# Expert slots in two phases: nine complete tiles of the first four groups, listed by GpSimd in step 15, run behind the last ranks

## The reference

```python
x = x + ga * attn(h)       # bidirectional state-space block: projection, causal convolution,
                           # scan over 2048 tokens forward and backward, gate, norm, out_proj
h = _layernorm(x) * (1 + cb) + sb
gate_logits = einsum('bsd,ed->bse', h, gate_w) + gate_b + expert_bias
top_idx = argmax(gate_logits, axis=-1)          # one of 8 experts per token
for e in range(8):
    mask = (top_idx == e)[..., None]
    y = relu(h @ w1[e] + b1[e]) @ w2[e] + b2[e]   # 128 -> 512 -> 128
    out = out + mask * y
x = x + gb * out
```

## Time and profile before

| | us |
|---|---|
| median of 3 runs | 446.13 (444.88 to 448.41) |
| the profiled execution's own time | 446.73 |
| its span in the trace | 444.8 |
| PE busy in the span | 400.8 (90%), 3156 instructions |
| DVE busy | 354.7 (80%) |
| ACT busy | 290.8 (65%) |
| POOL busy | 317.0 (71%) |

### The profile page before, as it was taken

The page is one execution under the profiler, slowest core; times in us unless marked ns, Lnnn a source line. Parts: engine busy times, 40 slices in busy tenths (PEclk is TensorE's granted clock), DMA queues, the critical chain, the costliest instruction groups (busy, mean ns, idle before and its releaser), DMA issues.

```text
span 444.8 us, 10736 instructions
## 1 busy us (share of the span) xinstructions
PE 400.8 (90%) x3156; PEld 364.5 (82%) x3156; DVE 354.7 (80%) x1064; ACT 290.8 (65%) x827; POOL 317.0 (71%) x478
## 2 busy tenths in 40 slices
PE   7898989997998899798998998999988699999990
PEld 7676878897898698587898887899877699999990
DVE  5758789998879999988889987996987078778781
ACT  3748699787699897787788789987420044444430
POOL 4744894899995989589898898697575245656662
PEclk9869999999999999999999999999999999999997
DMA  8999999999800000010101100031112578888740
GB/s 233 323 335 335 334 336 332 334 336 332 256 7 0 2 2 0 1 49 2 50 1 49 37 13 1 1 117 75 49 36 74 170 206 222 234 221 224 214 146 0
DMA packets 54856, 63.30 MB, mean 142 GB/s; under 512 B 4604, under 2 KB 47868, under 8 KB 54672
## 3 DMA queue, kind: packets, MB, share of 16 engines
q1 hardware_dynamic: 49808, 54.57, 41.4%
q0 software_dynamic: 2832, 6.50, 4.1%
q10 hardware_dynamic: 2160, 1.55, 1.3%
HBM read 20.97 MB, written 42.09 MB: 142 GB/s over the span
## 4 chain that ended last, share of the span: by engine, by line
PE 35%; DVE 17%; issue 12%; POOL 12%; ACT 10%; DMA 5%; SPq 5%; ACTq 2%; POOLq 0%; DVEq 0%
PE bank L1351 3%; PE bank L1302 3%; POOL out_dram L856 3%; PE bank L1367 3%; PE bank L1371 3%; PE bank L1344 3%; DVE bank L1778 3%; PE bank L1363 3%; POOL routed_rows L768 2%; PE bank L1329 2%; SPq L536 2%; POOL accb L637 2%; SPq L530 2%; DMA zs<-routed_rows 2%; PE bank L1335 2%
## 5 line engine op out<-in xcount | busy, mean ns | idle before, releaser
L637 POOL TENSOR_TENSOR accb<-accb,prod 128x512 f32<-128x512 f32 x48 | 61.3, 1278 | 29.2 <-ACT accb L949 25.5
L1778 DVE SCALAR_TENSOR_TENSOR bank<-raw,cw,bank 128x512 f32<-128x512 f32 x96 | 72.1, 751 | 2.3 <-ACT bank L959 0.9
L856 POOL DMA_INDIRECT out_dram<-raw x39 | 38.2, 979 | 34.3 <-POOL raw L851 12.8
L673 POOL TENSOR_SCALAR lseg<-strict,av 128x128 f32<-128x128 f32 x128 | 48.0, 388 | 6.8 <-DVE av L1737 4.8
L1351 PE MATMUL bank<-skip,cx 128*128 128x128 f32 x256 | 41.1, 283 | 7.0 <-DVE st L1824 6.6
L1212 ACT ACTIVATE raw<-bank 128x128 f32<-128x128 f32 x39 | 10.8, 278 | 53.4 <-PE bank L1575 47.8
L1239 PE MATMUL bank<-ones 128*128 128x128 f32 x266 | 38.8, 296 | 5.2 <-issue 2.7
L1603 PE MATMUL bank<-raw 128*128 x312 | 43.1, 282 | 0.0
L998 ACT ACTIVATE xt<-bank,dtv 128x128 f32<-128x128 f32 x128 | 39.5, 362 | 5.5 <-PE bank L1330 5.2
L768 POOL DMA_INDIRECT routed_rows<-rows,rowat x32 | 32.8, 1025 | 14.1 <-issue 8.6
L1351 PEld LDWEIGHTS bank<-skip,cx 128*128 128x128 f32 x256 | 33.6, 191 | 9.8 <-DVE st L1824 9.0
(11 more groups left out here) (238 smaller groups left out, 1148.4 us busy)
## 6 DMA issues: line engine op xcount, KB each, us to landing
routed_rows<-padrow SPq DMA_DIRECT2D x32, 1040.0 KB, 12.6
zs<-in_w_dram SPq DMA_DIRECT2D x35, 258.0 KB, 3.3
zs<-routed_rows SPq DMA_DIRECT2D x39, 130.0 KB, 3.2
raw<-in_w_dram SPq DMA_DIRECT2D x1, 2048.0 KB, 7.6
xs<-in_u_dram SPq DMA_DIRECT2D x3, 512.0 KB, 9.7
routed_rows<-padrow SPq DMA_DIRECT2D x8, 130.0 KB, 3.4
zs<-in_w_dram ACTq DMA_DIRECT2D x4, 258.0 KB, 4.6
out_dram<-raw POOLq DMA_INDIRECT x39
```

The lines of the kernel that those rows point to most:

```text
L637: pool.tensor_tensor(accb[:, :], accb[:, :], prod[:, :], ALU.add).then_inc(s_tapb, 1)
L673: last = pool.tensor_scalar(lseg[:, Q % LA, h, :], strict[:, d, :], av[:, b, col(d, h, t)], 1.0, ALU.mult, ALU.mult)
L856: pool.indirect_dma_start(out_rows, bass.IndirectOffsetOnAxis(ap=tok[:, s % 4, :].bitcast(mybir.dt.uint32), axis=0), ob[:, s % 4, :], None ...
L1778: dve.scalar_tensor_tensor(out=acc(S, g)[:, :], in0=raw[:, g, c0:c0 + BLK], scalar=cw[:, d, g, k:k + 1], in1=acc(S, g)[:, :], op0=ALU.mult ...
```

## The change

`FIRSTG` is 4 and `K1` is 9: of the 2048 tokens of groups 0 to 3, whatever the routing, at least ceil((2048 - 8 x 127) / 128) = 9 tiles of some expert are full. These nine tiles become slots 0 to 8 (first phase), the other 30 (`K2`) slots 9 to 38 (second phase).

- **POOL** gets `first_table()` in step 15, third chunk, ahead of `forward_norms(LASTG, 0, 2)`: 13 operations each of which waits for the one before (`link_first`) and three that don't, which list the nine tiles from `nextrow` as it stood after group 3. `table_constants` has six operations in place of three. `taken_tiles()`, five operations, stands between the last scatter of group 5 and those of group 6; it tells DVE's table which tiles are already taken. Behind the scatters POOL waits for all nine tiles of rows, copies their token numbers at once, and issues nine puts (`s_put1`) ahead of the 30 others.
- **SP** waits for `s_yz` as before, then for `s_firstv` and for the scatters of groups 0 to 3 alone, loads nine tiles of rows and, between them, w1 of slots 0 to 3, then w1 of slots 4 to 8. Then it waits for `s_tabv`, loads w1 of slots 9 to 12, waits for all scatters, and loads the rows of slot 9 and on. `RR` is 13. ACT issues no w1 any more.
- **PE** runs two `turn_rows` and four products of ones ahead of `ranks(7)`, then `hidden(0)` and slots 0 to 8, then waits for table and rows of slot 9, and goes on as before. The 44 products of ones of the three constants, and five ahead of `ranks(7)`, are gone. Slots 0 to 2 use one pair of PSUM banks (4, 5) for the hidden blocks; slot 3 and later ones alternate between two pairs. In the first phase the transposes and the sums of `down` share banks 0 and 3.
- **ACT** does all four hidden blocks of slots 0 to 8, and copies their sums to SBUF (`keep_sum`).
- **DVE** has a table of 30 slots in place of 39, and behind it works on the first nine outputs in wide operations (`first_gates`, `first_outputs(0, 4)` and `first_outputs(4, 9)`). It rectifies from slot 9 on.
- w1 lies in `hT` (three places) and `zs` (one), the nine sums and gates in `yzb`. The second `yT` transposes of group 7 use the alternating side banks in place of bank 0.

```diff
 # POOL, step 15
                     if j == 2:
+                        first_table()
                         forward_norms(LASTG, 0, 2)
                         scatter(g2)
...
             scatter(LASTG - 2, 3, BT)
+            taken_tiles()
             scatter(LASTG - 1)
             scatter(LASTG)
+            for s in range(K1):
+                hold(pool, s_rb[s], 16)
+            pool.tensor_copy(tok1, rr[:, 0:K1, 2 * DM:2 * DM + 1]).then_inc(s_tok, K1)
...
+            for s in range(K1):
+                put(s)
+            for s in range(K1, NSLOT):
                 token_numbers(s)
-                if s >= 1:
+                if s > K1:
                     put(s - 1)
 # POOL, the list (cut)
+            def first_table():
+                wide = [P, K1, NE]
+                first = prefix[:, 0, NE // 2:]
+                hold(pool, s_tab, NTAB0)
+                hold(pool, s_rt_dve, NR * (FIRSTG - 1) + 5)
+                link_first(pool.tensor_tensor(whole, nextrow[:, FIRSTG % 2, :], region_mid, ALU.subtract))
+                link_first(pool.tensor_scalar(whole, whole, 1.0 / P, ROUND, ALU.mult, ALU.add))
+                link_first(pool.tensor_scalar(first, whole, ROUND, 1.0, ALU.subtract, ALU.mult))
+                pool.tensor_scalar(coef[:, 0], first, -float(P), float(REGION), ALU.mult, ALU.add)
...
+                link_first(pool.tensor_tensor(behind1[:, 0], behind1[:, 1], coef[:, 0].unsqueeze(1).broadcast_to(wide),
+                                              ALU.mult))
...
+                pool.tensor_copy(slot_r[:, :, 0:K1], last).then_inc(s_firstv, 1)
 # SP
-            sp_.wait_ge(s_yz, NCH)
-            sp_.wait_ge(s_tabv, 1)
+            sp_.wait_ge(s_yz, CHUNKS + TPB + ZUSED)
...
+            sp_.wait_ge(s_firstv, 1)
+            landed(sp_, FIRSTG)
+            for s in range(K1):
+                first = first_row(s)
+                load_rows(s, first)
+                if s < RW:
+                    load_w1(s, first)
+            for s in range(RW, K1):
+                load_w1(s, first_row(s))
+            sp_.wait_ge(s_tabv, 1)
+            ahead = [first_row(s) for s in range(K1, K1 + 2)]
+            for s in range(K1, K1 + RW):
+                load_w1(s, ahead[s - K1] if s < K1 + 2 else first_row(s))
+            landed(sp_, B * NBLK)
             sp_.wait_ge(s_pad, 16)
             sp_.wait_ge(s_fresh[NFRESH], 16 * NE)
-            load_rows(0, first0)
...
+            for s in range(K1, NSLOT):
+                first = ahead[s - K1] if s < K1 + 2 else first_row(s)
                 load_rows(s, first)
-                load_w1(s, first)
+                if s >= K1 + RW:
+                    load_w1(s, first)
 # ACT
+            for s in range(NACT, K1):
+                if s + 1 < K1:
+                    rectify(s + 1, 0)
+                    if s + 2 < K1:
+                        rows_T(s + 2)
+                    rectify(s + 1, 1)
+                keep_sum(s)
 # PE
+            pe.wait_ge(s_firstv, 1)
             pe.wait_ge(s_yz, NCH - 1)
...
             logits(LASTG)
-            keep_warm(bank[4], 5)
-            ranks(LASTG)
-            keep_warm(bank[4], WARM_TABLE)
...
-            pe.wait_ge(s_tabv, 1)
-            keep_warm(bank[4], WARM_SCATTER)
...
-            keep_warm(bank[4], WARM_ROWS)
...
             turn_rows(0)
             turn_rows(1)
+            keep_warm(bank[4], 4)
+            ranks(LASTG)
             hidden(0)
-            for s in range(NSLOT):
+            for s in range(NPE, K1):
+                if s + 1 < K1:
+                    hidden(s + 1)
+                    if s + 2 < K1:
+                        turn_rows(s + 2)
+                down(s)
+            pe.wait_ge(s_tabv, 1)
...
+            turn_rows(K1)
+            turn_rows(K1 + 1)
+            hidden(K1)
+            for s in range(K1, NSLOT):
 # DVE
+            def first_outputs(s0, s1):
+                dve.wait_ge(s_yo2, s1)
+                link_early(dve.tensor_tensor(ob1[:, s0:s1, :], ob1[:, s0:s1, :], gsel1[:, s0:s1, :], ALU.mult))
+                dve.tensor_tensor(ob1[:, s0:s1, :], ob1[:, s0:s1, :], rr[:, s0:s1, DM:2 * DM], ALU.add).then_inc(s_ob, s1 - s0)
...
+            first_gates()
+            first_outputs(0, K1 // 2)
+            first_outputs(K1 // 2, K1)
+            rectify_high(K1)
```

More of the change, by code:

```diff
@@ L43 @@
 W1C = FF + FC
-RR = 6
+FIRSTG = 4
+K1 = -(-(FIRSTG * BLK - NE * (P - 1)) // P)
+assert 2 < K1 <= FIRSTG * BLK // P
+ROUND = 1.5 * 2.0 ** 23
+RR = 13
 RW = 4
+assert K1 <= RR
 B2K = 96
@@ L1194, in _, with rows_T, rectify, keep_sum @@
                         softplus_exp(nxt)
+            def rows_T(s):
+                act.wait_ge(s_eT, s + 1)
+                if s >= 2:
+                    act.wait_ge(s_h1, s - 1)
+                act.activation(hTs[:, s % 2, :], turn_bank(s)[:, 0:P], ACT.Copy).then_inc(s_eTc, 1)
+            def rectify(s, half):
+                act.wait_ge(s_h1a if half == 0 else s_h1, s + 1)
+                if s >= 2:
+                    act.wait_ge(s_y2, s - 1)
+                for f in range(half * FC // 2, (half + 1) * FC // 2):
+                    c0 = (f % 2) * P
+                    last = act.activation(hr[:, s % 2, f * P:(f + 1) * P], bank[high_low(s) + half][:, c0:c0 + P],
+                                          ACT.Relu, bias=w1t[s % RW][:, FF + f:FF + f + 1])
+                last.then_inc(s_hra if half == 0 else s_hrb, 1)
+            def keep_sum(s):
+                act.wait_ge(s_y2, s + 1)
+                act.activation(ob1[:, s, :], sum_bank(s)[:, 0:DM], ACT.Copy).then_inc(s_yo2, 1)
             out_T(LASTG, 0)
@@ L1534, in _, with turn_rows, hidden @@
                         sums(nxt)
+            def turn_rows(s):
+                pe.wait_ge(s_rb[s % RR], 16 * (s // RR + 1))
+                if s >= 2:
+                    pe.wait_ge(s_eTc, s - 1)
+                if 3 <= s < K1:
+                    pe.wait_ge(s_yo2, s - 2)
+                elif s in (K1, K1 + 1):
+                    pe.wait_ge(s_yo2, K1)
+                pe.transpose(turn_bank(s)[:, 0:P], rr[:, s % RR, 0:DM], ident[:, :]).then_inc(s_eT, 1)
+            def hidden(s):
+                pe.wait_ge(s_eTc, s + 1)
+                pe.wait_ge(s_w1[s % RW], 16 * (s // RW + 1))
+                if s == 0:
+                    pe.wait_ge(s_yz, NCH)
+                if s == 3:
+                    wait_free(pe, USE["o", LASTG, 0])
+                    wait_free(pe, USE["o", LASTG, 1])
+                for f in range(FC):
+                    if s not in (0, 3) and f == 0:
+                        pe.wait_ge(s_hra, same_banks(s) + 1)
+                    if s not in (0, 3) and f == FC // 2:
+                        pe.wait_ge(s_hrb, same_banks(s) + 1)
+                    c0 = (f % 2) * P
+                    mm = pe.matmul(bank[high_low(s) + f // 2][:, c0:c0 + P], w1t[s % RW][:, f * P:(f + 1) * P],
+                                   hTs[:, s % 2, :], start=True, stop=True)
+                    if f == FC // 2 - 1:
+                        mm.then_inc(s_h1a, 1)
+                mm.then_inc(s_h1, 1)
```

278 lines of the change are left out of this document (160 added, 118 removed).

## The result

The changed kernel took 449.29 us at the median (447.77 to 452.19, 8 runs), the kernel before 446.72 us beside it (8 runs, 444.88 to 453.27): ratio 1.0059, interval 1.003 to 1.0088. The forecast was 435.0 us, the range 432 to 440. It was wrong, by 14 us.

The account below looks back on a forecast made before the run. PE was taken to bound the 39 slots at 2.01 us each. First transpose of the rest +6.8 us, nine fewer slots behind it -18.1, net -11.3 from 446.73: 435.4, or 434.8 at the median, given as 435; range 432 to 440.

Parts of the forecast that it names:

- The pace of phase one: Slots 0 to 8: PE sets the pace at 2.01 us a slot; bounds 2.01 to 2.3, that is 0 to +2.
- rival B: Phase one slower, from w1 late beside the scatters or ACT falling behind: +2 to +4, about 438 us; chance 0.11.
- The joint between the phases: Before slot 9: rows queue behind SP's w1 of slot 12; PE stands 2.7 us, first transpose at 360.9.
- Rival D: At the joint, PE's clock falls to half during its stand: +5, 438 to 444 us; chance 0.10.
- GpSimd's list: Step 15 on POOL: `first_table` takes 5.4 to 5.6 us inside 5.82 us idle; taken as 0, bounds 0 to +1.
- rival C: Step 15: the list on POOL overruns its idle time because DVE holds it up, 436.5 to 439 us; chance 0.09.
- The sharing of banks at the start: Slots 0 to 2 share one pair of banks, so `hidden(1)` waits for ACT; costs about 1.5 us.
- w1 beside the scatters: Phase one's w1 loads arrive in time, 1.1 us to spare in the worse case; taken as nothing, bounds 0 to +3.
- A: Whole kernel: the forecast itself holds, 433 to 437.5 us; chance 0.60.
- F: At the joint: no stand, the rest starts at 358.2, 2.7 us better, 432.5 us; chance 0.03.
- G: Phase one: the nine slots wait for what they should run ahead of, work only moved, about 446 us; chance 0.03.
- E: Behind the joint: clock stays low, kernel slower by 1% from 8 half-clock slots, 455 us with ten; chance 0.04.

Follow-up runs that it names:

- value_early: Changed kernel with TensorE's load of the slot's expert number moved ahead of the transpose: 434.25 us, ratio 0.9751 to the kernel before.
- after: The changed kernel's own profiled execution, the slowest of its eight runs: 452.19 us, span 450.5; median 449.29 us, ratio 1.0059 to the kernel before.
- again: The changed kernel, unchanged, measured once more beside the kernel before: 438.94 us, ratio 0.9854.
- both_2: The program of both, unchanged, in another set of runs, a quiet set: 430.88 us, ratio 0.9671 to the kernel before.
- value_early_2: The program of value_early, unchanged, in a late set: 448.65 us, ratio 1.0034 to the kernel before.
- fill_joint: value_early with nine products of the constant block on TensorE behind `down(8)`: 446.28 us, ratio 0.998 to the kernel before.
- quiet set: Runs measured together, no kernel waiting over 0.5 us on "remote", with more DMA landing records (3209 to 3338); kernel before 444.6, 444.8 and 445.7 us.
- late set: Runs measured together, all but the kernel before waiting over 0.5 us on "remote", with fewer DMA landing records (2111 to 2226); kernel before 447.8 and 448.6 us.
- both: value_early with the rows of slots 9 to 12 all issued ahead of their four w1, in a late set: 447.59 us, ratio 1.0018 to the kernel before.
- both_swap: both with GpSimd's `first_table()` moved behind the last group's two norms and ahead of the scatter: 454.99 us, ratio 1.0171 to the kernel before.
- spaced: both with one GpSimd addition ahead of each of the last eight scatters and the nine puts issued one per slot: 443.27 us, ratio 0.9898.
- before_2: The kernel before, unchanged, run for its trace in a late set: 449.93 us (one run).

## Why the prediction was wrong

Four points of TensorE's timeline cut the forecast and the traces into the same pieces, in us. The forecast's transpose of slot 8 is its end of `down(8)`, 358.2, less the 4.2 us that lie between the two in value_early.

| | hidden(0) at | to transpose 8 | to transpose 9 | to the end | span |
|---|---|---|---|---|---|
| forecast | 338.7 | 15.3 | 6.9 | 72.6 | 433.5 |
| after | 340.9 | 24.2 | 9.1 | 76.3 | 450.5 |
| again | 338.2 | 18.2 | 7.8 | 74.5 | 438.6 |
| value_early | 336.6 | 15.3 | 7.0 | 73.8 | 432.6 |
| both_2 | 337.3 | 15.2 | 4.7 | 72.5 | 429.7 |
| value_early_2 (late) | 338.5 | 22.8 | 9.3 | 75.3 | 445.9 |

**The step that failed first is "The pace of phase one".** It said that PE needs 2.01 us a slot, and bounded the pitch by 2.01 to 2.3. The queue of matrix instructions was counted; the sequencer's was not. The load of the expert number had always been there at no cost. The change put a wait ahead of it, and I asked what is queued behind that wait only among the products. Measured: 2.50 to 2.65 us a slot, 2.9 us over the stretch (15.3 to 18.2), and nothing once the load moved ahead of the wait. That was rival B's size (+2 to +4), with another cause than the two it named: neither w1 nor ScalarE's load was late.

**"The joint between the phases" was right, and incomplete.** SyncE's order, the rows' DMA as releaser and a stand of 2.7 us (measured 2.78 in after, 3.12, 2.76) came as written. Rival D, given 0.10, came on top of it in each of the nine kernels that stood there for 2.7 to 3.3 us with nothing to fill the stand: half clock behind it. From transpose 9 to transpose 13 both_2 takes 5.7 us at full clock, value_early 7.3 and again 8.4 (364.14 to 372.58). So it costs 1.7 us where it lasted 3.4 us (value_early) and 2.8 us where it lasted 6.8 us (again), and 1.3 and 2.0 us by the time from transpose 9 to the end, where D had +5. TensorE: Matmul & The Clock Gate (the Trainium skill, What's actually happening) put it under 1% of a span; 0.4 to 0.6% is measured, and the trace agrees. My evidence against D, the stretch from 350 to 354, was sound as a reading: the kernel before had stood there for 2.67 us, as long as at the joint, and kept the clock.

```profile
351.76 1.58 PE L1239 MATMUL bank<-ones 128*128 128x128 f32 x12 [2.67 <-issue]
```

It misled as a forecast for the joint, where all nine were followed by half clock; what makes the difference is not shown. With products of ones in the stand (fill_joint, one execution) the clock stayed.

In a quiet set these two terms nearly close the account. again's span is 5.1 us over the forecast's 433.5: 2.9 in phase one, 0.9 up to transpose 9 (0.5 one more load, 0.4 a longer stand), 1.9 behind it, less 0.5 at `hidden(0)`. value_early, which has the pitch right, lies 0.9 under 433.5 and inside the range, but that is luck: its `hidden(0)` came 2.1 us early, for a cause that no run shows. both_2 lies 3.8 under, 2.2 of it the stand that the forecast had counted in and 1.4 at `hidden(0)`.

**The larger part of the miss in the measurement itself was in no step and no rival.** The forecast put the delay of TensorE's signals to ScalarE and VectorE at what a quiet trace shows, everywhere. Of the 17.0 us by which the profiled span exceeds 433.5, 2.3 were there at `hidden(0)`. Of 8.9 us up to transpose 8, the pitch explains 2.9 by again; 6 are the wait on "remote" and the half clock from 347.7 to 354.5 behind it. Two more such waits (1.55 us ahead of 367.75, 3.03 ahead of 381.62) fall in the last two pieces. value_early against value_early_2 prices the same thing without the pitch: 13.3 us of span, 14.4 us of the median, of which the kernel before shows 3.9 too. With both steps mended the forecast would still have failed in a late set: both took 447.59 us there.

What is shown of it: it comes in some sets and not in others, on one and the same chip; it comes where GpSimd issues indirect DMAs some 1.27 us apart, scatters or puts; leaving the eight scatters out took their wait away (8.3 us), and setting them 1.73 us apart or more did too, with as many DMAs. The spacing alone does not make it: the quiet sets have the same 1.27 us and no late signal. The kernel before issues the same eight beside products of ones, and its puts 2.01 us apart, and it is slower in late sets by 2 to 4 us only. What the change gains, it gains by moving work that needs signals into just this stretch.

What stays open is why only some sets have it. They are the ones whose recordings lose the most records, and all runs here are recorded. NOTIFIC — the notification-queue block (the Trainium skill, 7.1 Overflow) says that a full internal record queue holds back its producer rather than lose a record. That would fit stalled products that wait for nothing, but no run here is without recording, so it is not shown; nor is it that unrecorded runs are free of it.

**The other terms.** GpSimd's list costed at 5.4 to 5.6 us took 5.4 and overran its idle time by some 0.5 us, where the forecast took 0 with bounds 0 to +1; rival C did not come. both_swap shows what the list would have cost outside. The sharing of banks at the start, w1 beside the scatters, free outputs: value_early's 15.3 us agree with their sum. Rivals A, F and G fell; E's sign came, by a mechanism that was not E's: half clock behind the joint lasted 3.4 or 6.8 us and never the 32 us that E needs. The longest in phase one or two was 10.2 us (360.4 to 370.6), in spaced behind late signals.

## What to carry to other kernels

When an edit puts a semaphore wait ahead of other instructions on an engine, list everything behind it up to the first user of its result, the sequencer's register loads too: one such load cost 0.5 us a slot, and moving one line gave it back. At a joint between two loops issue first what is wanted first, for as many buffers as are free, and price a stand of TensorE like those of this joint (2.7 to 3.3 us) at its own length plus up to 2.8 us of half clock; the kernel before kept its clock over a gap of 2.67 us, so this part is a risk and not a certainty. A stretch where an engine runs products that nobody reads hides more than idle time; it may be the one stretch in which signals are slow, and a kernel that moves real work there should be timed in more than one set.

## What the runs showed that was not expected

- A signal from TensorE to ScalarE took up to 5.3 us (value_early_2: a transpose done at 342.57, its copy at 347.87), and arrived near the end of a row of eight indirect DMAs some 1.27 us apart (0.1 to 0.7 us off in the six late traces that have this row); at 1.73 us apart or more (spaced) none was late. VectorE's signals were late too, beside puts 1.27 us apart: a wait of 4.93 us in both.
- In one of the same sets (before_2) TensorE stopped for 1.17 and 1.05 us within products that wait for nothing.
- The ratio of one unchanged program ran from 0.985 to 1.006, of another from 0.975 to 1.003, and of a third (both) from 0.967 to 1.002, between sets. Each had an interval of some half a per cent to either side.
